# Attention plus int8 feed-forward on one core: queries stored once, 112-row transposes of the probabilities, score matmuls still 128 stationary columns wide

## What is computed

```python
def _L0_attn_ref(x, wq, wk, wv, wo):            # 16 heads, 4 kv heads, head size 128
    q, k, v = x @ wq.T, x @ wk.T, x @ wv.T      # x: (16, 256, 256) after layernorm
    scores = einsum('bhtd,bhsd->bhts', q, k_full) / sqrt(128)
    mask = (k <= q) & ((k < 4) | (k >= q - 31))  # 4 sink keys and a window of 32
    attn = softmax(scores where mask)
    return einsum('bhts,bhsd->bhtd', attn, v_full).reshape(...) @ wo.T
x = x + _L0_attn_ref(_layernorm(x), wq, wk, wv, wo)
x = x + _L0_ffn_ref(_layernorm(x), weight, bias)  # int8-quantised 256 x 256 linear layer
```

## Time and profile before

| what | value |
|---|---|
| median of three executions | 605.4 us |
| the profiled execution: its own time | 607.0 us |
| its span, first to last instruction | 605.1 us |
| granted TensorE clock, mean | 0.989 of full speed |
| busy share of the span: PE, DVE, ACT, POOL | 98%, 89%, 66%, 52% |

### The profile page before, as it was taken

How to read it: one execution, slowest core, us unless ns; L and a number is a source line. 1 busy time by engine, 2 the same in 40 slices (tenths; PEclk the granted TensorE clock), 3 DMA queues, 4 the chain that set the end, 5 groups by cost and what they waited for, 6 DMA issues and landing times.

```text
span 605.1 us, 18063 instructions
## 1 busy us (share of the span) xinstructions
PE 593.6 (98%) x7556; PEld 524.7 (87%) x7556; DVE 536.3 (89%) x1072; ACT 401.0 (66%) x633; POOL 313.6 (52%) x310
## 2 busy tenths in 40 slices
PE   8999999999999999999999999999999999999995
PEld 7779888898988989888898988989898898988983
DVE  7899999898988979899898989979899898879987
ACT  7898665676666666666667566567666666666673
POOL 2155364555646455564646647455564645646473
PEclk8899999999999999999999999999999999999997
DMA  8748042150604316060250604216060330505001
GB/s 305 236 89 192 2 110 51 61 116 19 159 15 94 69 38 140 19 134 25 72 105 20 157 19 105 56 42 135 20 140 2 92 68 36 125 19 121 21 3 52
DMA packets 36272, 49.69 MB, mean 82 GB/s; under 512 B 2784, under 2 KB 22240, under 8 KB 36192
## 3 DMA queue, kind: packets, MB, share of 16 engines
q1 hardware_dynamic: 36048, 48.41, 32.6%
q10 hardware_dynamic: 144, 0.13, 0.1%
HBM read 35.42 MB, written 12.58 MB: 79 GB/s over the span
## 4 chain that ended last, share of the span: by engine, by line
PE 92%; DVE 5%; ACT 1%; issue 1%; DMA 0%; POOL 0%; DVEq 0%; POOLq 0%
PE ps L416 27%; PE ps L538 26%; PE ps L447 8%; PE ps L395 7%; PE ps L384 6%; PE ps L491 5%; PE ps L521 5%; PE ps L520 5%; PE ps L372 1%; PE ps L584 1%; PE ps L553 1%; DVE Qs L1070 1%; PE ps L569 1%; DVE pool L1097 0%; DMA X<-in_L_attn_x 0%
## 5 line engine op out<-in xcount | busy, mean ns | idle before, releaser
L416 PE MATMUL ps<-xT,WqT 128*128 128x256 f16 x1536 | 181.6, 275 | 1.0 <-DVE Qs L1070 0.7
L538 PE MATMUL ps<-WoT,pool 128*128 128x256 f16 x1440 | 167.3, 273 | 0.2 <-DVE pool L1097 0.2
L416 PEld LDWEIGHTS ps<-xT,WqT 128*128 128x128 f16 x1536 | 148.3, 99 | 18.6 <-DVE Qs L1070 1.0
L538 PEld LDWEIGHTS ps<-WoT,pool 128*128 128x128 f16 x1440 | 138.4, 98 | 15.4 <-DVE pool L1097 0.3
L1504 POOL TENSOR_TENSOR small<-E,rr 128x576 f32<-128x576 f32 x64 | 73.7, 1152 | 109.5 <-DVE rr L1092 109.3
L892 ACT ACTIVATE pool<-ps 128x512 f16<-128x512 f32 x128 | 70.2, 594 | 82.0 <-PE ps L521 82.0
L818 ACT ACTIVATE Qs<-ps 128x576 f16<-128x576 f32 x128 | 82.7, 646 | 43.7 <-PE ps L416 43.7
L1510 POOL TENSOR_TENSOR PP<-small,PP 128x576 f16<-128x576 f32 x64 | 82.0, 1282 | 52.6 <-ACT PP L879 52.6
L1070 DVE TENSOR_TENSOR Qs<-ps,Qs 128x576 f16<-128x576 f32 x128 | 92.8, 728 | 4.0 <-ACT Qs L818 4.0
L1493 POOL TENSOR_TENSOR Sm<-Sm,mx 128x576 f32<-128x576 f32 x64 | 73.7, 1152 | 36.1 <-DVE mx L1083 34.7
L1097 DVE SCALAR_TENSOR_TENSOR pool<-ps,pool 128x512 f16<-128x512 f32 x128 | 82.3, 681 | 0.2
(11 more groups left out here) (134 smaller groups left out, 893.5 us busy)
## 6 DMA issues: line engine op xcount, KB each, us to landing
values<-Vn SPq DMA_DIRECT2D x32, 256.0 KB, 2.0
VW<-values SPq DMA_DIRECT2D x16, 480.0 KB
big<-values SPq DMA_DIRECT2D x16, 480.0 KB
X<-in_L_attn_x SPq DMA_DIRECT2D x16, 256.0 KB, 8.4
VW<-values SPq DMA_DIRECT2D x16, 240.0 KB
big<-values SPq DMA_DIRECT2D x16, 240.0 KB
out<-pool SPq DMA_DIRECT2D x15, 256.0 KB, 6.0
big<-in_L_attn_wq SPq DMA_DIRECT2D x4, 512.0 KB, 8.0
```

What stands on the lines that cost most here:

```text
L416: a = pe.matmul(banks[BANK_Q[f]][:, j * 256:j * 256 + 256], WqT[:, k, wl, h * 128:h * 128 + 128], xT[:, b % 2, k, xl, :], start=(n == 1), ...
L538: a = pe.matmul(out_view(b, t), OT[:, p, ol, h, t * 128:t * 128 + 128], WoT[:, 4 * g + h, wl, :], start=first, stop=(end and g == KV - 1), ...
```

## The change

`Qs` gets 1024 columns: step 0 keeps 4 x 32 queries, steps 1 to 8 hold 4 x 28 = 112 each, every query once. A step owns what its columns hold, so `p_transpose` runs forward, with 128 rows for step 0 and 112 for the others, and writes only the step's own columns. `scores` still takes 128 stationary columns for steps 0 to 7: for steps 1 to 7 the last 16 are the first 16 columns of the next step, and the 16 output rows they give are masked and not transposed. Step 8 has nothing behind it and takes 112. `q_views` now covers steps 1 to 8 of two heads; `q_first_views` copies step 0 of all four heads in one piece, on ACT and on DVE, once both banks are filled, with semaphores `qs_h` and `qs_l` of their own. ACT's copy waits for `q_low(u, 0)`, and `q_low(u, 1)` waits for ACT's copy.

```diff
--- before.py
+++ after.py
@@ -36,6 +36,11 @@
 
 def q0_of(s):
     return 0 if s == 0 else STEP * s + 4
+def step_rows(s):
+    return 4 * (q0_of(s + 1) - q0_of(s))
 
 
 def output_pieces(j):
@@ -92,7 +97,7 @@
         xn = sb("xn", [128, 2, D], F32)
         xhl = sb("xhl", [128, 2, 2, D], F16)
         xT = sb("xT", [128, 2, 2, 2, T], F16)
-        Qs = sb("Qs", [128, 2, 2, NT * 128], F16)
+        Qs = sb("Qs", [128, 2, 2, 4 * T], F16)
         Kw = sb("Kw", [128, 2, KV, 2, 8, KEYS], F16)
         Vn = sb("Vn", [128, 2, 2, 512], F16)
         VW0 = sb("VW0", [128, 8, 2, 512], F16)
@@ -156,6 +161,8 @@
         cst_ok, ln_st, ln_xn, xt_ok = sem("cst_ok"), sem("ln_st"), sem("ln_xn"), sem("xt_ok")
         osc_ok, esc_ok = sem("osc_ok"), sem("esc_ok")
         k_l, v_l, q_l = sem("k_l"), sem("v_l"), sem("q_l")
+        qs_h, qs_l = sem("qs_h"), sem("qs_l")
         s_m, s_mx, p_r = sem("s_m"), sem("s_mx"), sem("p_r")
         pt_ok, o_l = sem("pt_ok"), sem("o_l")
         f_x2, f_st, f_xn, f_s, f_xr, f_xq = (sem("f_x2"), sem("f_st"), sem("f_xn"), sem("f_s"),
@@ -217,10 +224,16 @@
         b_v = bass.AP(bias_d.tensor, bias_d.offset, [[0, 128], [1, D]])
 
         def q_views(p, f):
-            src = bass.AP(ps, 512 * BANK_Q[f], [[4096, 128], [256, 2], [STEP, NT], [1, 32]])
-            dst = [bass.AP(Qs, ((p * 2 + l) * NT * 128) + 64 * f, [[4 * NT * 128, 128], [32, 2], [128, NT], [1, 32]])
+            src = bass.AP(ps, 512 * BANK_Q[f] + 32, [[4096, 128], [256, 2], [STEP, NT - 1], [1, STEP]])
+            dst = [bass.AP(Qs, (p * 2 + l) * 4 * T + 128 + 2 * STEP * f, [[16 * T, 128], [STEP, 2], [4 * STEP, NT - 1], [1, STEP]])
                    for l in range(2)]
             return src, dst
+        def q_first_views(p):
+            src = bass.AP(ps, 512 * BANK_Q[0], [[4096, 128], [256, 4], [1, 32]])
+            return src, [Qs[:, p, l, 0:128].rearrange("p (h q) -> p h q", h=4) for l in range(2)]
 
         def k_bank(b, f):
             return BANK_F if (b, f) == (0, 0) else BANK_KV
@@ -401,6 +414,7 @@
                 if u:
 
                     pe.wait_ge(q_l, 2 * (u - 1) + f + 1)
+                    pe.wait_ge(qs_l, u)
                 if b == 0:
                     pe.wait_ge(w_l[f"q{g}"], f + 1)
                 if f == 0 and g == 0:
@@ -421,6 +435,7 @@
                 b, g = divmod(u, KV)
                 p = u % 2
                 pe.wait_ge(q_l, 2 * u + 2)
+                pe.wait_ge(qs_l, u + 1)
                 if g in (0, 2):
                     pe.wait_ge(k_l, 2 * b + g // 2 + 1)
                 for c, (s0, s1) in enumerate(CHUNKS):
@@ -443,9 +458,11 @@
                         f_free(u - 1)
                     for s in range(s0, s1):
                         w = max(s - 1, 0)
+                        rows = 128 if s < NT - 1 else 4 * STEP
                         for n, (ql, kl) in enumerate(PAIRS):
-                            a = pe.matmul(banks[BANK_S[c]][:, (s - s0) * KEYS:(s - s0 + 1) * KEYS],
-                                          Qs[:, p, ql, s * 128:s * 128 + 128], Kw[:, b % 2, g, kl, w, :],
+                            a = pe.matmul(banks[BANK_S[c]][0:rows, (s - s0) * KEYS:(s - s0 + 1) * KEYS],
+                                          Qs[:, p, ql, 4 * q0_of(s):4 * q0_of(s) + rows], Kw[:, b % 2, g, kl, w, :],
                                           start=(n == 0), stop=(n == 2))
                     a.then_inc(s_ps, 1)
 
@@ -487,8 +504,10 @@
                 else:
                     pe.wait_ge(s_m, u + 2)
                 v = half(pt_bank(u), F16).rearrange("p (h q) -> p h q", h=4)
-                for s in reversed(range(NT)):
-                    a = pe.transpose(v[:, :, STEP * s:STEP * s + 32], PP[:, p, s].rearrange("p l k -> p (l k)"), idh[:, :])
+                for s in range(NT):
+                    rows = step_rows(s)
+                    a = pe.transpose(v[:, :, q0_of(s):q0_of(s + 1)], PP[0:rows, p, s].rearrange("p l k -> p (l k)"),
+                                     idh[0:rows, 0:rows])
                 a.then_inc(pt_ps, 1)
 
             def pv(u, j):
@@ -502,6 +521,7 @@
                 if u == NU - 3:
 
                     pe.wait_ge(q_l, 2 * (NU - 1) + j + 1)
+                    pe.wait_ge(qs_l, NU)
                 elif u > NU - 3:
 
                     pe.wait_ge(o_l, 2 * u + j - 3)
@@ -615,6 +635,7 @@
                 a.then_inc(wf_ps, 1)
 
                 pe.wait_ge(q_l, 2 * 9 + 1)
+                pe.wait_ge(qs_l, 10)
                 pe.matmul(banks[0][:, 0:256], ones[:, :], diag[:, :, :].rearrange("p t o -> p (t o)"),
                           start=True, stop=True).then_inc(wf_ps, 1)
 
@@ -816,6 +837,11 @@
                 src, dst = q_views(u % 2, f)
                 act.wait_ge(q_ps, 2 * u + f + 1)
                 act.activation(dst[0], src, ACT.Copy).then_inc(q_h, 1)
+                if f:
+                    src, dst = q_first_views(u % 2)
+                    act.wait_ge(q_l, 2 * u + 1)
+                    act.activation(dst[0], src, ACT.Copy).then_inc(qs_h, 1)
 
             def exps(u):
                 p = u % 2
@@ -1067,7 +1093,13 @@
             def q_low(u, f):
                 src, dst = q_views(u % 2, f)
                 dve.wait_ge(q_h, 2 * u + f + 1)
+                if f:
+                    dve.wait_ge(qs_h, u + 1)
                 dve.tensor_tensor(dst[1], src, dst[0], ALU.subtract).then_inc(q_l, 1)
+                if f:
+                    src, dst = q_first_views(u % 2)
+                    dve.tensor_tensor(dst[1], src, dst[0], ALU.subtract).then_inc(qs_l, 1)
 
             def s_mask(u):
                 p = u % 2
@@ -1615,12 +1647,13 @@
     m = np.full((128, NT, KEYS), -1.0e38, np.float32)
     for s in range(NT):
         k0 = STEP * max(s - 1, 0)
-        for i in range(32):
-            q = STEP * s + i
+        n = step_rows(s) // 4
+        for i in range(n):
+            q = q0_of(s) + i
             keys = list(range(4)) + list(range(k0, k0 + 60))
             for c, k in enumerate(keys):
                 if k <= q and (c < 4 or (k >= 4 and k >= q - WIN + 1)):
-                    m[i::32, s, c] = 0.0
+                    m[i:4 * n:n, s, c] = 0.0
     eye = np.eye(128, dtype=np.float32)
     return m, eye
 
```

## The result

The changed kernel takes 620.55 us (median of six executions, 619.23 to 624.54) against 605.65, the median of six executions of the kernel before beside it: ratio 1.0251, 95% interval 1.023 to 1.0272. It is 14.9 us slower. The forecast had the sign and one tenth of the size.

The account below looks back on a forecast made before the run. PE's queue was taken to bound the steady part. Transposes -3.5, scores +3.8, ACT and DVE 0 and the two ends +1.0 gave +1.3 us on 605.4, about 606.7 us, with a range of 605.0 to 607.2.

Parts of the forecast that it names:

- What bounds the kernel: Steady part: PE's queue sets the time, busy all 450.00 us; DVE and ACT cost nothing if in time.
- Transposes, -3.5 us: 512 of 576 transposes go from 128 to 112 moving columns, 55.6 to 48.8 ns each: -3.5 us.
- Scores, +3.8 us: Step 8's 192 score matmuls load 112 stationary columns the plain way, 49 ns instead of 29.3: +3.8 us.
- the reading of two passes in a float32 record: Score loads: each float32 record holds two passes, so a plain 112-column load takes 44 to 49 ns.
- ACT and DVE under cover: Query copies: DVE 23 and ACT 58 ns more a unit, hidden behind PE in the steady part, costing nothing.
- The two ends, +1.0 us: Start and end: queries arrive later, scores(1) by 0.6 us and the end by 0.4; range 0.3 to 1.5.
- the unnamed case: Whole kernel: something not listed among the forecast and its rivals happens; chance 0.04.
- The fourth, DVE as the bound: Steady part: late ACT copies make PE wait 0.1 us a turn, about +5, 612 us; chance 0.03.
- The 614 us rival: Step 8's scores: a narrow load takes a whole float32 record, 88 ns, +8.8, 614.2 us; chance 0.08.

Follow-up runs that it names:

- e5: Changed kernel with step 0 copied bank by bank and Qs padded to 128 columns a step, so all score loads are wide: 603.14 us, ratio 0.9963.
- e3: Kernel before, with step 8's three score matmuls on 112 stationary columns, last 16 rows left out (output wrong): 609.29 us, ratio 1.0057.
- e4: Changed kernel with Qs at 128 columns a step, all score loads wide, step 0 still copied for all four heads at once: 616.65 us, ratio 1.0169.
- e6: Changed kernel with 34 matmuls of 256 columns into an unused bank, placed in PE's wait ahead of q_fill(4, 0): 617.62 us.
- e7: Kernel before, with one wait made later: q_fill(4, 0) also waits for q_low(3, 1): 610.9 us, ratio 1.008.
- e8: Kernel before, with q_fill(4, 0) also waiting for q_low(3, 1) and 34 matmuls put into that wait: 609.31 us, ratio 1.0049.
- e2: Kernel before, no width changed, three waits (q_fill, feed-forward weight scales, pv of unit 61) made to need both q_low: 619.02 us, ratio 1.0211.
- e1: Changed kernel with step 0 copied bank by bank, without qs_h and qs_l, widths unchanged: 606.61 us, ratio 1.001 to the kernel before.

## Why the prediction was wrong

*What bounds the kernel: right.* PE's queue sets the time of the steady part, 450.00 of 450 us busy after (from 110 to 560 us) as before.

*Transposes, -3.5 us: right.* 0.45 us for nine, 49 ns each; the 112-row load keeps its 97 ns. e5 shows 49 ns a unit, 3.2 us over all.

*Scores, +3.8 us: right in kind, a little small.* The title's "still 128 stationary columns wide" holds for 24 of a unit's 27 score matmuls; the other three are the cost. The turn's 27 matmuls went from 0.79 to 0.85 us, and 22.4 ns a narrow load in e3 make 52 ns from start to start, where I took 49 from a range of 44 to 49; 192 of them are 4.3 us. That follows the reading of two passes in a float32 record, which no row had shown by itself. By the Trainium skill ("TensorE: Matmul & The Clock Gate", "Weight-path perf modes — Fast Weight Load (FWL) and DoubleRow") only 128 weights that are not float32 load fast, and the trace agrees: records of 98 against 132 ns. The Trainium skill's section "LDWEIGHTS" on the same page gives P/1.2 ns, by estimate 93 ns for 112 columns, which does not hold here: the measured 52 stands. Together the two terms gave +18 ns a unit, 0.92 us from unit 9 to 60 and 1.2 over 64 units, where I had +0.3.

*ACT and DVE under cover: right where it looked.* 599 and 540 ns, forecast 600 and 539. No wait on `Qs` came up between units 10 and 60.

*The two ends, +1.0 us: here it failed.* The step asked when `scores` gets its queries. That part was about right: `scores(1)` followed `scores(0)` after 6.53 us, before 5.87, +0.66 where 0.6 was forecast, and +0.85 between profiles with no halved clock ahead of it (6.97 in e4 and e6, 6.12 in e7 and e8). But the queries' PSUM banks have a second customer. The diff adds `pe.wait_ge(qs_l, u)` to `q_fill(u, f)`, and the prediction never priced it. It even named the 0.7 us for which `q_fill(3, 0)` waited, and took it for a wait for `q_low(2, 0)` still; behind the change it is one for the small copy that stands after `q_low(2, 1)`, and three times as long. Before, then after:

```profile
31.96 1.48 PE L416 MATMUL ps<-xT,WqT 128*128 128x256 f16 x12 [0.72 <-DVE Qs L1070]
```

```profile
32.19 1.47 PE L430 MATMUL ps<-xT,WqT 128*128 128x256 f16 x12 [2.02 <-DVE Qs L1099]
```

In the steady part `q_fill(t+1)` stands behind `scores(t)`, which has waited for the same thing, so the new wait is free; I read the steady order and carried that over. In the order written out for the first units, PE reaches `q_fill(4, 0)` before DVE reaches `q_low(3, 1)`: it uses bank 0 while DVE still owes bank 1. One instruction that reads both banks takes that away. The same holds at `q_fill(5, 0)` and `q_fill(6, 0)` (1.5 us), at the feed-forward weights (1.7) and at `q_fill(63, 0)` (1.3). With `q_fill(3, 0)` (1.2) and `q_fill(4, 0)` (6.9) the turns with such a wait are longer by 12.6 us, of which the clock is 2.8; in e2 the same turns are longer by 11.6. The order rows that I showed of DVE were of the right queue, but the place was units 0 and 1, and the largest wait was at units 3 and 4.

*Luck.* e1 has the change's widths and its added instructions without the late handover, and is 1.2 us above the kernel before; the sum forecast +1.3. That nearness is partly luck: the widths cost 0.9 us more than forecast, and the ends, in e1, about as much less.

*Rivals.* None of them was what happened; it was the unnamed case, to which I gave 0.04. The fourth, DVE as the bound, named the right engine, but it looked for a recurring wait in the steady part. The 614 us rival would have come nearest in time for a wrong reason.

## What to carry to other kernels

When a copy is changed to read two PSUM banks at once, list every instruction that may next write either bank, and look up each one's place in the program's order, the prologue and the end first: here the new wait was free in the steady part and cost time only at the two ends and at the feed-forward weights. A wait that is free in 50 turns can cost more in a handful of others than a width does in all. And where the matmuls are short, pad the stationary operand to 128 columns, also where a step fills only 112: with the handover mended, the layout that stores nothing twice saved no time (e1, 606.61 us), the padded one did (e5, 603.14).

## What the runs showed of the hardware

A float16 load of 112 stationary columns costs 52 ns from start to start behind matmuls of 64 columns, one of 128 columns 29.3 or less (0.79 us for 27). Loads of 112 rows show the same 97 to 98 ns as loads of 128, and the transposes behind them start 49 ns apart. In the changed kernel a wait of 3.9 us cost 2.9 us more through TensorE's clock, which was granted at half for 6.8 us behind it, and 34 matmuls put into the wait won that back. How long the clock stayed at half differed from kernel to kernel: 6.8 us in the changed kernel and in e2, 3.4 in e7, though the waits ahead of it differed by at most 0.1 us (3.91, 3.99 and 3.99). What sets that length no run shows.
